# Moving four folded query pieces to the end of each head, and GpSimd's key sum behind a tile's second subtraction

## The reference, cut to what matters

```python
kv_c = _linear(x, d_kv_w, d_kv_b)
k_c = _linear(kv_c, u_k_w, u_k_b).reshape(b, s, H, Dh)
k_r = _linear(kv_c, qr_w, qr_b).reshape(b, s, H, Dr)
v = _linear(kv_c, u_v_w, u_v_b).reshape(b, s, H, Dh)
q_c_lat = _linear(x, d_q_w, d_q_b)
q_c = _linear(q_c_lat, u_q_w, u_q_b).reshape(b, s, H, Dh)
q_r = _linear(q_c_lat, qr_w, qr_b).reshape(b, s, H, Dr)
q_r, k_r = rope(q_r), rope(k_r)
q = concatenate([q_c, q_r]); k = concatenate([k_c, k_r])
probs = softmax(q @ k.T * scale)
ctx = (probs @ v).reshape(b, s, H * Dh)
return _linear(ctx, out_w, out_b)
```

## Time and profile before

| | |
|---|---|
| median of three runs | 2477.97 us (2475.82 to 2478.64) |
| the profiled execution | 2481.38 us |
| its span | 2480.0 us |
| VectorE busy | 2152.9 us, 87% |
| TensorE matmul busy | 2207.0 us, 89% |
| ScalarE busy | 1822.3 us, 73% |
| GpSimd busy | 1074.5 us, 43% |
| second attention, first shift to last | 827.0 to 2283.9 us |

### The profile page before, as it was taken

The page is one execution under the profiler, slowest core; times in us unless marked ns, Lnnn a source line. Parts: engine busy times, 40 slices in busy tenths (PEclk is TensorE's granted clock), DMA queues, the critical chain, the costliest instruction groups (busy, mean ns, idle before and its releaser), DMA issues.

```text
span 2480.0 us, 50650 instructions
## 1 busy us (share of the span) xinstructions
PE 2207.0 (89%) x18456; PEld 1587.4 (64%) x18544; DVE 2152.9 (87%) x3182; ACT 1822.3 (73%) x2608; POOL 1074.5 (43%) x1480
## 2 busy tenths in 40 slices
PE   4888888879987899999999999999999999988899
PEld 2444444446555577777777767767767777766687
DVE  6888888769996999999999999999999999987422
ACT  4877777735545688888888888888888888877411
POOL 3312112102223566656656656656656656622200
PEclk9999999979998899999999999999999999999899
DMA  3000000050000699999999999999999999999100
GB/s 128 1 2 2 2 1 1 2 116 1 1 1 1 107 186 188 195 191 189 197 190 191 196 190 190 195 191 190 193 192 195 189 191 193 200 193 191 34 18 17
DMA packets 1119318, 300.69 MB, mean 121 GB/s; under 512 B 1107232, under 2 KB 1116416, under 8 KB 1118208
## 3 DMA queue, kind: packets, MB, share of 16 engines
q1 hardware_dynamic: 1116224, 295.21, 69.1%
q10 hardware_dynamic: 2848, 2.23, 0.3%
HBM read 18.45 MB, written 2.10 MB: 8 GB/s over the span
## 4 chain that ended last, share of the span: by engine, by line
DVE 28%; PE 20%; issue 9%; DMA 5%; ACT 5%; DVEq 0%; SPq 0%; ACTq 0%
DVE parts L1652 13%; DVE lows L1636 12%; DMA partsT<-parts 5%; PE psS L1587 3%; PE psOb L1507 3%; PE psS L1490 2%; PE psS L1492 2%; PE psS L1491 2%; ACT parts L1836 2%; PE psOb L1543 1%; PE psOb L1508 1%; ACT prob L1826 1%; PE psOb L1607 1%; PE psPb L1607 1%; DVE shift L1644 1%
## 5 line engine op out<-in xcount | busy, mean ns | idle before, releaser
L1826 ACT ACTIVATE prob<-psS,shift 128x1024 f32<-128x1024 f32 x512 | 574.1, 1121 | 171.5 <-DVE shift L1644 161.8
L1652 DVE TENSOR_TENSOR parts<-prob,parts 128x1024 f16<-128x1024 f32 x512 | 661.0, 1291 | 23.1 <-ACT parts L1836 19.7
L1636 DVE TENSOR_REDUCE lows<-psS 128x1 f32<-128x1024 f32 x512 | 621.8, 1214 | 4.9 <-PE psS L1492 4.7
L1836 ACT CAST parts<-prob 128x1024 f16<-128x1024 f32 x512 | 536.6, 1048 | 24.3 <-DMA partsT<-parts 20.5
L1490 PE MATMUL psS<-k_hi,q_lo 128*128 128x512 f32 x1024 | 450.4, 440 | 101.2 <-ACT prob L1826 94.2
L1507 PEld LDWEIGHTS psOb<-kv,partsT 128*128 128x128 f16 x4096 | 357.0, 97 | 94.3 <-issue 75.2
L1507 PE MATMUL psOb<-kv,partsT 128*128 128x130 f16 x4096 | 397.3, 221 | 16.2 <-DMA partsT<-parts 16.0
L1491 PE MATMUL psS<-k_lo,q_hi 128*128 128x512 f32 x1024 | 407.2, 398 | 0.0
L1492 PE MATMUL psS<-k_hi,q_hi 128*128 128x512 f32 x1024 | 406.6, 397 | 0.0
L1508 PE MATMUL psOb<-kv,partsT 128*128 128x66 f16 x4096 | 387.2, 193 | 0.0
L1508 PEld LDWEIGHTS psOb<-kv,partsT 128*128 128x128 f16 x4096 | 360.5, 98 | 1.0 <-issue 1.0
(11 more groups left out here) (296 smaller groups left out, 4003.2 us busy)
## 6 DMA issues: line engine op xcount, KB each, us to landing
partsT<-parts SPq DMA_TRANSPOSE x512, 4.8
ef<-in_ewT SPq DMA_DIRECT2D x1, 2048.0 KB, 10.9
rf<-in_rwT SPq DMA_DIRECT2D x1, 2048.0 KB, 10.1
outw_s<-in_outwT SPq DMA_DIRECT2D x1, 2048.0 KB, 8.6
trig<-in_trig SPq DMA_DIRECT2D x2, 1024.0 KB, 11.3
out_x<-ot SPq DMA_DIRECT2D x16, 128.0 KB, 1.7
wug<-in_wupT SPq DMA_DIRECT2D x4, 256.0 KB, 4.0
wug<-in_wgateT SPq DMA_DIRECT2D x4, 256.0 KB, 3.5
```

The source lines that it names most:

```text
L1636: dve.tensor_reduce(lows[:, n % 2, g:g + 1], psS[:, (2 * n + g) % 3, :], AX_X, ALU.min).then_inc(half_min, 1)
L1652: dve.tensor_tensor(parts[:, s, 1, :], prob[:, g, :], parts[:, s, 0, :], ALU.subtract).then_inc(low_done, 1)
L1826: act.activation(prob[:, g, :], psS[:, (2 * n + g) % 3, :], ACT.Exp, bias=shift[:, n % 2:n % 2 + 1], scale=-1.0).then_inc(exp_done, 1)
L1836: act.copy(parts[:, s, 0, :], prob[:, g, :]).then_inc(high_done, 1)
```

## The change

A folded piece leaves tiles 2, 5, 8 and 11 and goes to tiles 12 to 15, with its matmuls, its `fold` and its `rest`. The counts in the waits follow the new order (`place_of`, `rotated_by`, `rested_by`). The scores wait for one group's `rest` at every fourth tile instead of for all four at a head's first tile. `whole` stays in its tile; `whole_k` moves into a function of its own, `add_keys`, called one tile later, ahead of that tile's wait for the first subtraction (so right behind the second subtraction of the tile before, and behind the add into `x`). The bias of the fold is read from `beta` itself, and the copy `beta_h`, its semaphore and one of nine counts disappear. `load_small` is issued four tiles later.

```diff
         def piece_at(n):
             i = n % NT
-            return i if i < 12 and n // NT + 1 < NH else None
+            if n // NT + 1 == NH or (i < 12 and i % 3 == 2):
+                return None
+            return i if i < 12 else 3 * (i - 12) + 2
+
+        def place_of(head, piece):
+            if head == 0:
+                return piece
+            j, kind = divmod(piece, 3)
+            return 2 * j + kind if kind < 2 else 8 + j
 
         def rotated_by(head, p):
-            return 8 * head + 2 * (p // 3) + min(p % 3, 2)
+            return 8 * head + min(p, 8) if head else 2 * (p // 3) + min(p % 3, 2)
 
         def rested_by(head, p):
-            return 4 * head + p // 3
+            return 4 * head + max(p - 8, 0) if head else p // 3
...
                 if head and i == 0 and g == 0:
                     pe.wait_ge(rests_done, sums(head + 1, 0))
-                    pe.wait_ge(rested, 4 * (head + 1))
+                if head and i % 4 == 0 and g == 0:
+                    pe.wait_ge(rested, 4 * head + i // 4 + 1)
...
             def fold(head, piece, halves_scored):
-                act.wait_ge(piece_ready, 12 * head + piece + 1)
-                act.wait_ge(weights_in, 9 * (head + 1))
+                act.wait_ge(piece_ready, 12 * head + place_of(head, piece) + 1)
                 if halves_scored:
                     act.wait_ge(score_ready, halves_scored)
                 act.activation(q_hi[latent, slot, :], piece_bank(head, piece)[latent, :], ACT.Identity,
-                               bias=beta_h[latent, 0:1]).then_inc(folded, 1)
+                               bias=beta[latent, head:head + 1]).then_inc(folded, 1)
...
             def take_weights(head):
-                pool.wait_ge(piece_ready, 12 * head)
-                pool.wait_ge(rested, 4 * head)
+                pool.wait_ge(piece_ready, 12 * head - (4 if head > 1 else 0))
                 place_weights(head)
-                pool.tensor_copy(beta_h[latent, :], beta[latent, head:head + 1]).then_inc(weights_in, 1)
-                pool.wait_ge(weights_in, 9 * head + 9)
...
-                for side, (out_rows, rows) in enumerate(((whole, rotary), (whole_k, latent))[:2 if head else 1]):
-                    pool.tensor_tensor(out_rows[rotary, :], rot[0][rows, :], rot[1][rows, :], ALU.add).then_inc(added_up, 1)
-                    pool.wait_ge(added_up, sums(head, j) + side + 1)
+                pool.tensor_tensor(whole[rotary, :], rot[0][rotary, :], rot[1][rotary, :], ALU.add).then_inc(added_up, 1)
+                pool.wait_ge(added_up, sums(head, j) + 1)
+
+            def add_keys(head, j):
+                pool.tensor_tensor(whole_k[rotary, :], rot[0][latent, :], rot[1][latent, :], ALU.add).then_inc(added_up, 1)
+                pool.wait_ge(added_up, sums(head, j) + 2)
...
                 add(n - LATER - 1)
+                if ahead and 3 <= i <= 12 and turn == 1:
+                    add_keys(head, j)
                 if ahead and i == 14 and head + 1 < NH:
                     take_weights(head + 1)
                 if n < TILES:
                     pool.wait_ge(low_done, 2 * n + 1)
...
-                if n == TILES - NT - 3:
+                if n == TILES - NT + 1:
                     load_small()
```

More of the change, by code:

```diff
@@ L1035, in second_attention @@
         filled, weights_in = sem("b_filled"), sem("b_weights")
-        beta_h = sb(L, "beta_h", [P, 1])
         def place_weights(head):
-            done = 9 * head
+            done = 8 * head
             for r in range(2):
@@ L1069, in prepare @@
             cleared, bt_high, bt_rest, bt_mid = sem("l_cleared"), sem("l_bt_high"), sem("l_bt_rest"), sem("l_bt_mid")
-            qr_low, bt_low, offset = sem("l_qr_low"), sem("l_bt_low"), sem("l_offset")
+            qr_low, bt_low = sem("l_qr_low"), sem("l_bt_low")
             def tensor():
@@ L1215, in vector @@
                 dve.wait_ge(small_ready, 1)
-                dve.tensor_scalar(beta[latent, :], psP[0:C, D:D + NH], -SCALE, None, ALU.mult).then_inc(offset, 1)
+                dve.tensor_scalar(beta[latent, :], psP[0:C, D:D + NH], -SCALE, None, ALU.mult)
                 dve.tensor_tensor(bias_row[:, :], psP[:, 0:D], outb_s[:, :], ALU.add)
@@ L1294, in gpsimd @@
                 place_weights(0)
-                pool.wait_ge(offset, 1)
-                pool.tensor_copy(beta_h[latent, :], beta[latent, 0:1]).then_inc(weights_in, 1)
-                pool.wait_ge(weights_in, 9)
             vector()
@@ L1448, in project @@
                 cols = slice(j * BANK, (j + 1) * BANK)
-                before = piece if head else piece - 5
+                before = place_of(head, piece) if head else piece - 5
                 if before > 0 or head:
@@ L1454, in project @@
                 bank = piece_bank(head, piece)
-                pe.wait_ge(weights_in, 9 * (head + 1))
+                pe.wait_ge(weights_in, 8 * (head + 1))
                 if kind < 2:
@@ L1614, in rotate @@
                 cols = slice(j * BANK, (j + 1) * BANK)
-                dve.wait_ge(piece_ready, 12 * head + piece + 1)
+                dve.wait_ge(piece_ready, 12 * head + place_of(head, piece) + 1)
                 if 4 * head + j:
@@ L1625, in rest @@
                 dve.wait_ge(folded, 4 * head + piece // 3 + 1)
-                dve.scalar_tensor_tensor(out=q_lo[latent, slot, :], in0=piece_bank(head, piece)[latent, :], scalar=beta_h[latent, 0:1],
+                dve.scalar_tensor_tensor(out=q_lo[latent, slot, :], in0=piece_bank(head, piece)[latent, :],
+                                         scalar=beta[latent, head:head + 1],
                                          in1=q_hi[latent, slot, :].bitcast(F32), op0=ALU.add,
```

## The result

The changed kernel takes 2486.64 us (median), against 2478.06 us before. The ratio is 1.0032, with a 95% interval of 1.0019 to 1.0045: 8.6 us slower. One execution in six of each kernel was far slower (2520.52 us before, 4878.50 us after): it counts in the medians and not in the ratio. The forecast was 2490, slower, with a range of 2470 to 2502.

What follows compares the result with a forecast made beforehand. VectorE's time per tile in the second attention was taken as the bound; +1.6 us a pair gave +11 over 7 pairs, +12 with head 0, so the median went from 2477.97 to 2490, range 2470 to 2502.

Steps and rivals of the forecast that it cites:

- A pair of heads: An odd head (zero change) and an even head (+1.6 us) in the second attention, together forecast to cost +1.6 us.
- +0.90: Tail tiles 12 to 15 gaining a folded piece: +0.90 us each without an output, +0.42 with one, to 5.88.
- T+0.95: Tiles 2, 5, 8 without output: `whole_k` starts 0.95 us after the second subtraction's end (T), 0.11 to 0.22 ahead of VectorE.
- the tile would take 5.90: Tiles losing the folded piece, no output added: period 5.90 us, before 6.21, a gain of 0.31.
- the tile behind pay 0.34 and 0.50: Behind a tile with an output, the second subtraction loses 0.34 us and the next first subtraction 0.50, together 0.84.
- its own 0.37: Around a folded piece on VectorE: 0.37 us extra from the piece itself, even without GpSimd beside it.
- rival 2: The folded piece's 0.37 us is GpSimd's doing: tail tiles 5.51, total -10, 2468 us; 7 in 100.
- Rival 1: GpSimd comes second: `whole_k` starts after VectorE's subtraction, tiles without output stay at 4.98; -8, 2470 us; 13 in 100.
- rival 3: No change: the tile behind an output loses only 0.34 or only 0.50 us; 2479 to 2482; 20 in 100.
- rival 4: Costlier: ScalarE bounds tiles 12 and 13 (6.2 us against 5.88); 2499, up to 2505; 12 in 100.
- The sum gave +12: Whole kernel: heads 1 to 14 as 7 pairs make +11 us, head 0 as half a pair, together +12.
- the stall moved and unchanged: Last heads: the small loads hold SP for 3.36 us; their stall moves with them unchanged, plus or minus 3.

Runs made afterwards that it cites:

- the pieces alone: The changed kernel with the key sum `whole_k` back in its old tile, the folded pieces staying in tiles 12 to 15: 2468.7 us, ratio to before 0.9964.
- the sum behind the context ops: The kernel before, pieces in their old tiles, the key sum in its old tile but behind GpSimd's three small context ops: 2460.56 us, ratio 0.9934.
- half the sum: The changed kernel with the key sum adding only the first 256 of 512 columns: 2462.57 us, ratio to before 0.9941.
- the sum alone: The kernel before with only the key sum moved behind the second subtraction, pieces in their old tiles: 2486.16 us, ratio 1.0039.
- the loads later: The kernel before with only the five small loads issued four tiles later: 2478.2 us, ratio 1.0003.

## Why the prediction was right, and where it was off

**The bound and the measure.** VectorE's periods were the right measure. A pair of heads, forecast at +1.6, costs +1.6: odd heads went from a mean of 90.83 to 91.47 (+0.64, forecast 0.0) and even ones from 90.77 to 91.74 (+0.97, forecast +1.6). Heads 1 to 13 sum to 1190.74 us against 1180.41, +10.3, where 6.5 pairs of the forecast make +10.4. The split within a pair was off and cancels: the last period of a tail lies behind the next head's first shift, so that an odd head holds one tail period of its even neighbour (+0.90) in place of one of its own (+0.42), 0.48 of the 0.64.

**Step by step.** That `whole_k` would start at T+0.95 and win by 0.11 to 0.22: it won by 0.21. That the tile would take 5.90: 5.91. That with an output GpSimd would come second and the tile behind pay 0.34 and 0.50: 0.33 and 0.51. That the folded piece costs its own 0.37 wherever it stands: the three steps are the same with GpSimd idle, which puts rival 2 out. The Trainium skill's rule of the held instruction (page VectorE: DVE Perf Modes, section Two Vector instructions with no wait between them) agrees with this trace in all three steps, 0.25, 0.79 and 0.20. The Trainium skill's rule of the lock (page SBUF — State Buffer, section Who interferes with whom) agrees with the experiments: order decides who waits (the pieces alone, the sum behind the context ops), and the length of the holder decides for how long (half the sum). Rival 1 didn't come about; rival 3 is out since both losses are there; rival 4 is out, since tail tiles stay within 0.13 of 5.88 (the one of 6.39 holds the forecast 0.50). It was priced too high from the start: ScalarE's 4.9 us a tile is a mean that already holds the four folds and the roundings of a head, which the prediction added once more.

**The term that was mis-sized.** The sum gave +12, the medians +8.6 (4.7 to 11.2 by the interval), and the two profiled executions +2.8: one was 3.3 above its median, the other 2.5 below. So differences of a few us between single executions carry nothing unless other kernels repeat them. Head 0 was counted at +0.8 and took 90.67 against 90.87, -0.2. Heads 14 and 15 were counted as ordinary, with the stall moved and unchanged; they sum to 180.6 against 185.6. The stretch ahead of the first shift was 2.1 shorter (824.9 against 827.0). The change takes the first copy into `beta_h` and its wait out of that stretch, but in the traces it is 824.9 to 826.5 us with the pieces in the tail and 825.0 to 827.5 with them in their old tiles, so an effect can't be told from chance. The term that was mis-sized is the one of the last two heads, forecast at +1.6 and measured at -5.0. The stall round the small loads was let stand unchanged and shrank: its two periods in the kernel before (7.93 and 8.46) are 6.4 over 4.98 each, its four in the changed kernel (6.09 to 6.59) are 5.1. Most of the 5.0, 4.1 us, is in one place, which other kernels do repeat: the period behind the last shift but one. VectorE's last two shifts, before and after:

```profile
2274.11 0.21 DVE L1644 TENSOR_SCALAR shift<-lows 128x1 f32<-128x1 f32 x1
...
2283.90 0.21 DVE L1644 TENSOR_SCALAR shift<-lows 128x1 f32<-128x1 f32 x1
```

```profile
2281.26 0.21 DVE L1650 TENSOR_SCALAR shift<-lows 128x1 f32<-128x1 f32 x1
...
2286.91 0.21 DVE L1650 TENSOR_SCALAR shift<-lows 128x1 f32<-128x1 f32 x1
```

9.79 us became 5.66. The waits around it (us in total, times, longest) say for what, before and after:

```profile
PEld psOb L1507 <- DMA partsT<-parts: 3.5, 1, 3.5
```

```profile
PEld psOb L1512 <- DMA partsT<-parts: 1.2, 2, 1.0
```

TensorE waited 3.5 us for one transpose of the probabilities. The wait has a second price, which three stretches of 5 us show (two of before, one of after; columns as in the first table):

```profile
2270.00:2275.00 5.00, 2.51 (x23) 1.77 (x22) 4.16 (x5) 2.70 (x5) 1.60 (x4) 1.00 1.37 158
2275.00:2280.00 5.00, 4.09 (x27) 3.48 (x28) 1.29 (x2) 3.37 (x5) 0.09 (x1) 0.66 0.99 206
2278.00:2283.00 5.00, 4.17 (x48) 3.38 (x47) 4.25 (x6) 4.27 (x6) 1.61 (x4) 1.00 1.17 238
```

TensorE was busy for only 2.51 of 5 us, and behind that its granted clock was 0.66: part of the stretch ran at the lower level of 1.2 GHz, and 27 matmuls filled 4.09 us, where at 1.00 in the changed kernel 48 took 4.17. The same period is 9.79, 8.99, 8.79 and 8.90 in the four kernels with the pieces in tiles 2 to 11 (before, the sum alone, the loads later, the sum behind the context ops), and 5.66, 5.68, 5.95 and 5.66 in the four with the pieces in the tail. The longest wait for a transpose there is 3.5, 2.9, 2.6 and 3.1 us in the first four, each with a fallen clock (0.66 to 0.77 over the 5 us behind the last shift but one), and 1.0 to 1.8 us at a clock of 1.00 in the other four. So it goes with the pieces' place, through no piece of that head, which has none. How the place decides when a landing is late stays open: I tried only the small loads, and they aren't it. The other sizes of the last heads differ by chance or by the same unknown. Heads 0 to 15 together come to +5.1 in the two traces, within the interval of the medians; the forecast of +12 lies just above it.

## What to carry to other kernels

Where two engines exclude each other, ask of each op who is issued first and what the other is then kept from; moving an op buys nothing unless it lands where the other engine does something that doesn't need the shared access for as long as the op lasts. A change of several parts can hide a good one: here the pieces in the tail bring 8 us and the moved sum takes 17. Before placing an op, write down the gaps of the engine that sets the time (here 1.06 us from the end of a second subtraction to the next first one) and the order in which the other engine reaches them; a lead of 0.1 us decided 1 us.

## What the runs showed of the hardware

- Whichever of GpSimd and VectorE's subtraction is first holds on for its whole length: an add of 1.29 us stretched a subtraction from 1.21 to 2.16 us, one of 0.73 us to 1.60 us. The blocked op begins 0.12 to 0.15 us before the holder's recorded end.
- How large a recorded lead has to be can be read from all subtractions of the second attention in the eight traces. With a GpSimd op recorded 0.06 to 0.12 us ahead, VectorE never went first. At 0.04 and 0.05 either did, and at 0.00 to 0.03 VectorE went first in 150 of 157 cases, as here in the kernel before, where the last GpSimd op on the context takes 1.38 in place of 0.31. So a lead of 0.05 us or less can't be relied on:

```profile
1008.85 1.38 POOL L1966 TENSOR_TENSOR ctxp<-both_sums,ctxp 128x64 f16<-128x64 f32 x1
1008.86 1.21 DVE L1652 TENSOR_TENSOR parts<-prob,parts 128x1024 f16<-128x1024 f32 x1
```

- The folded piece on partitions 64 to 127 costs VectorE 1.03 us for 0.76 us of recorded work (0.25 + 0.79 + 0.20, less the 0.21 which shift and `rden` take without it), since the op itself and the next two start only after the end of the one before (0.03 us after it).
- Five small loads issued between transposes cost 4.9 to 6.7 us over the periods of 4.98 around them, wherever they stood: in five traces as two periods of 7.4 to 9.2, with TensorE's granted clock at 0.5 for part of them, in three as four periods of 5.9 to 6.7 at a clock of 1.00. Moving them didn't change the time of the kernel.
